# Graph and int8 layers on one core: another way to the quantising maximum, and the next layer's first half among the int8 products

## The chip, the core and the metric

One core of a Trainium2 chip runs the whole program. The number that counts is the device time of one execution in microseconds; three runs of a kernel are timed and their median is given. The profile is of one further execution, taken by the hardware profiler.

## What is computed

The model has four residual steps over 625 rows of 1024 numbers, with 20625 graph edges:

```
x = x + gnn0(layernorm(x))      # relational graph layer, 8 relations, tanh gate
x = x + ffn0(layernorm(x))      # int8 layer, below
x = x + gnn1(layernorm(x))      # h = x @ W.T + b, then a normalised sum over neighbours
x = x + ffn1(layernorm(x))      # top-2 mixture of 8 experts and a shared one
```

The change touches the second step and the start of the third. The second is

```
x_scale = max(abs(x2).max() / 127.0, EPS)            # one maximum over all 625 x 1024
x_int8  = clip(round(x2 / x_scale), -128, 127)
out     = (x_int8 @ weight_int8.T) * x_scale * weight_scale.T + bias
```

so no product of this step can begin before the maximum over all rows of the normalised input is known.

## The kernel before

The 625 rows lie in five chunks (c = 0 to 4) of P = 125 partitions. Each engine has its own program, and `on.wait_ge(*at(event))` waits for a named event of another. An engine works strictly in the order of its program.

**Weights.** Weight tiles (128x512) come in groups of four through two staging buffers (`load`, on SP). ScalarE writes the high part of each tile into a ring of RT = 10 places (`highs(to)`, line 339), and VectorE or, for the tiles in `pool_lo`, GpSimd writes the low part (`lows(to)`, line 349). A group is loaded when the high and low parts of the group two before it exist. A place of the ring is filled again when the product that used it is done. A product in full precision is three matmuls for each of eight tiles (`three`, line 493): 24 for one chunk and one half of the columns. G0 is the first tile of the third step, S1 = G0 + 16 the first of the shared expert.

**PSUM.** Eight banks are handed out in turn by `Banks.take`: the next one that is not held. The one who takes a bank waits for the event that the last user named when it took it. `by_chunk` takes its five banks at its start.

**Gate and norm.** Half 1 of the gate product runs chunk by chunk on TensorE. VectorE takes out each chunk (line 1353), adds it to X (1356), gathers statistics (1164, 1169), takes the row maximum of the chunk before (`row_max`, 1346), and makes the shift of the norm in five one-column steps (`finish`, 1174 to 1183). ScalarE takes the root (899) and writes the normed chunk into U (905); chunk 4's is written by VectorE (1187). GpSimd adds the layer's bias to X after each norm (1807).

**Maximum.** VectorE reduces the five row maxima to a column (1369), TensorE turns the column to a row (606), VectorE reduces the row (1371), TensorE spreads the result over the partitions (612), VectorE makes scale and inverse (1373, 1375).

**Quantising.** ScalarE casts seven of the eight int8 weight tiles to bf16 (1032), once the gate product is done; GpSimd casts the first (1812). VectorE (chunks 0, 2) and ScalarE (1, 3, 4) multiply by the inverse and add a large number that rounds ("q magic", 1379 and 1036); VectorE subtracts it and limits (1382). TensorE turns the chunk in bf16 (623), VectorE writes it to xqT (1387).

**Int8 products.** TensorE runs the chunks' two halves (640). VectorE scales the result (1399), GpSimd adds it to X (1819; chunk 4 on VectorE, 1405), VectorE makes the statistics and the shift of the next norm ("n3"), ScalarE the norm. From chunk 2 on, TensorE turns the normed chunk c - 2 (483); ScalarE writes the high part of the turned chunk (913) and VectorE the low part (1194).

**Third step.** Half 0 of its product (`gnn`, 0) runs by chunk with the turns of chunks 3 and 4 after chunks 0 and 1; then half 1. VectorE takes out each chunk (`g_out`, 1419 and 1422), with ScalarE between (1051), in order of half and chunk, and begins with it after it has made the low parts up to G0 + 17. Then comes the sum over neighbours (668).

## Time and profile before

| | us |
|---|---|
| median of three runs | 1204.71 |
| lowest, highest | 1201.17, 1207.81 |
| the profiled execution | 1205.84 |
| span of its instructions | 1204.1 |

| engine | busy us | share of the span |
|---|---|---|
| TensorE, matmuls | 1111.2 | 92% |
| VectorE | 704.0 | 58% |
| GpSimd | 450.8 | 37% |
| ScalarE | 378.4 | 31% |

Times are microseconds from the start of the span. In the profile PE is TensorE, PEld its loading of weights, DVE VectorE, ACT ScalarE, POOL GpSimd and SP the engine that issues most of the transfers. L1346 is line 1346 of the kernel. "x3" behind a row is the number of instructions that it merges; the time before it is then from the start of the first to the end of the last. A bracket gives how long the engine stood idle before the row and who released it. The granted clock is a share of TensorE's full speed: 1.00 is 2.4 GHz, 0.50 is 1.2 GHz.

### The profile page before, as it was taken

What the parts mean: (1) busy time and instruction counts of PE and PEld (TensorE: products, weight loads), DVE (VectorE), ACT (ScalarE), POOL (GpSimd) and SP (SyncE); (2) the same over time, 40 slices, a digit from 0 to 9 for tenths busy, and PEclk for the clock granted to TensorE, in tenths of its full rate; (3) what the DMA queues carried; (4) which work ended last, traced back from release to release, by engine and by line L of the source; (5) the groups of instructions that cost most, each with busy time, mean ns of one, the idle gap of its engine ahead of it and who ended that gap; (6) DMA issues with size and microseconds to landing.
All of it is one profiled execution on the core that took longest, in us unless ns stands there. A gap on an engine that the chain in (4) does not pass through costs nothing.

```text
span 1204.1 us, 14335 instructions
## 1 busy us (share of the span) xinstructions
PE 1111.2 (92%) x5483; PEld 919.2 (76%) x5483; DVE 704.0 (58%) x1350; ACT 378.4 (31%) x591; POOL 450.8 (37%) x306
## 2 busy tenths in 40 slices
PE   4579999999999999999999999989968997989895
PEld 3467777777777777777799999977746775777773
DVE  6257666665566662121167767666967467656547
ACT  3022222222322222222133233243253324037552
POOL 6006564665556457740033212206544002410006
PEclk9889999999999999999999999989879999978997
DMA  9945577786766556575455663738411102566857
GB/s 351 408 142 142 143 163 195 194 206 190 181 165 148 128 118 146 114 139 190 155 185 170 200 178 105 245 125 210 140 35 53 70 2 72 203 219 232 261 167 244
DMA packets 88179, 202.78 MB, mean 168 GB/s; under 512 B 29383, under 2 KB 45354, under 8 KB 79528
## 3 DMA queue, kind: packets, MB, share of 16 engines
q1 hardware_dynamic: 37962, 129.17, 33.7%
q0 software_dynamic: 32016, 35.50, 13.7%
q10 hardware_dynamic: 18126, 37.13, 10.2%
q8 instruction: 46, 0.75, 0.3%
q14 instruction: 29, 0.24, 0.1%
HBM read 142.37 MB, written 59.39 MB: 168 GB/s over the span
## 4 chain that ended last, share of the span: by engine, by line
PE 80%; DVE 7%; DMA 4%; ACT 2%; issue 1%; POOL 0%; POOLq 0%; DVEq 0%; SPq 0%
PE ps L493 70%; DMA stage<-in_w_e 4%; PE ps L739 3%; PE ps L702 2%; DVE rl L349 1%; PE ps L668 1%; PE ps L750 1%; ACT rh L339 1%; PE ps L685 1%; DVE st L1164 1%; DVE xTl L1194 1%; PE ps L717 1%; ACT EOs L1119 1%; PE ps L483 0%; DVE X L1607 0%
## 5 line engine op out<-in xcount | busy, mean ns | idle before, releaser
L349 DVE TENSOR_TENSOR rl<-stage,rh 128x512 fp32r<-128x512 f32 (+1 forms) x274 | 227.0, 860 | 324.9 <-ACT rh L339 321.2
L493 PE MATMUL ps<-rh,xTh 128*125 128x512 f32 x880 | 351.1, 399 | 24.0 <-DVE xTl L1194 20.0
L339 ACT CAST rh<-stage 128x512 fp32r<-128x512 f32 (+1 forms) x288 | 194.3, 707 | 533.7 <-PE ps L493 310.9
L493 PE MATMUL ps<-rl,xTh 128*125 128x512 f32 x880 | 349.6, 397 | 0.0
L1755 POOL DMA_INDIRECT adj_scratch<-cnt,idx x162 | 266.8, 1647 | 219.0 <-DMA adj_scratch<-cnt,idx 61.2
L493 PE MATMUL ps<-rh,xTl 128*125 128x512 f32 x880 | 347.8, 395 | 0.0
L493 PEld LDWEIGHTS ps<-rh,xTh 128*125 128x125 f32 x880 | 164.4, 187 | 67.7 <-DVE xTl L1194 20.9
L493 PEld LDWEIGHTS ps<-rh,xTl 128*125 128x125 f32 x880 | 164.5, 187 | 42.5
L493 PE MATMUL ps<-rh,Ar 125*125 125x342 f32 x600 | 190.3, 322 | 6.0 <-issue 6.0
L493 PEld LDWEIGHTS ps<-rl,xTh 128*125 128x125 f32 x880 | 164.2, 187 | 40.2
L493 PE MATMUL ps<-rl,Ar 125*125 125x342 f32 x600 | 189.9, 322 | 0.0
L1213 DVE SCALAR_TENSOR_TENSOR EQ<-KR,kc,later 128x768 bf16<-128x768 f32 x162 | 154.3, 1017 | 0.0
L493 PEld LDWEIGHTS ps<-rh,Ar 125*125 125x125 f32 x600 | 113.0, 188 | 6.2 <-issue 6.1
L493 PEld LDWEIGHTS ps<-rl,Ar 125*125 125x125 f32 x600 | 113.0, 188 | 0.0
L1770 POOL TENSOR_TENSOR Atot<-Atot,Ar 128x3125 f32<-128x3125 f32 x7 | 45.4, 6483 | 100.2 <-ACT Ar L935 100.1
L1287 DVE SCALAR_TENSOR_TENSOR U<-ps,rc,U 125x342 f32<-125x342 f32 (+1 forms) x120 | 66.2, 570 | 27.1 <-PE ps L493 24.8
L982 ACT COPY He<-ps 125x512 f32<-125x512 f32 x80 | 46.9, 586 | 30.1 <-PE ps L493 16.5
L349 POOL TENSOR_TENSOR rl<-stage,rh 128x512 fp32r<-128x512 f32 x14 | 17.5, 1273 | 83.8 <-ACT rh L339 83.8
L1194 DVE TENSOR_TENSOR xTl<-ps,xTh 128x500 fp32r<-128x500 f32 x30 | 18.9, 672 | 33.5 <-ACT xTh L913 33.5
L483 PE MATMUL ps<-ident,U 125*128 125x125 f32 x160 | 21.6, 280 | 16.0 <-POOL dms L1736 10.9
L493 PE MATMUL ps<-rh,uTh 128*125 128x512 f32 x80 | 33.5, 419 | 3.0 <-DVE rl L349 2.9
L702 PE MATMUL ps<-xeh,rh 128*128 128x196 f32 x128 | 35.5, 277 | 0.6 <-DVE xel L1588 0.6
(263 smaller groups left out, 1217.4 us busy)
## 6 DMA issues: line engine op xcount, KB each, us to landing
stage<-in_w_rel SPq DMA_DIRECT2D x32, 1024.0 KB, 6.6
stage<-h_scratch SPq DMA_DIRECT2D x24, 855.0 KB, 6.3
stage<-in_w_e SPq DMA_DIRECT2D x16, 1024.0 KB, 6.8
adj_scratch<-Z POOLq DMA_DIRECT2D x16, 767.0 KB, 24.1
KR<-key_scratch ACTq DMA_DIRECT2D x27, 384.0 KB, 3.6
h_scratch<-He ACTq DMA_DIRECT2D x40, 257.0 KB, 9.7
h_scratch<-He ACTq DMA_DIRECT2D x40, 256.0 KB, 8.9
stage<-in_w_gate SPq DMA_DIRECT2D x8, 1024.0 KB, 6.5
```

What stands on the lines that cost most here:

```text
L339: e.copy(h, s).then_inc(*a_hi.up(*[("hi", t) for t in step(i)]))
L349: e.tensor_tensor(l, s, h.bitcast(F32), ALU.subtract).then_inc(*own.up(*[("lo", t) for t in step(i)]))
L483: ins = e.transpose(ps[:, b, j * P:(j + 1) * P], source[:, c, k * 128:(k + 1) * 128], ident[0:P, 0:P])
L493: ins = e.matmul(ps[0:P, b, 0:width], a, m, start=first and n == 0, stop=last and n == len(parts) - 1)
L702: ins = e.matmul(ps[:, b, 0:vn], a[:, ws], m[:, k, v0:v0 + vn], start=k == 0 and j == 0, stop=k == 7 and j == 2)
L739: ins = e.matmul(ps[0:HC, b, :], a, m, start=k == 0 and q == 0, stop=k == 1 and q == 2)
L982: e.copy(He[0:P, s % NHE, 2:514], ps[0:P, banks.of["unit", unit, hf, c], :]).then_inc(*a_out.up(("he", unit, c, hf)))
L1194: e.tensor_tensor(l, ps[:, b, 0:4 * P].rearrange("p (k n) -> p k n", k=4), h.bitcast(F32), ALU.subtract).then_inc(*v_out.up((name, "lo", c ...
L1213: e.scalar_tensor_tensor(out=EQ[:, j, :], in0=KR[:, g % 4, :], scalar=kc[:, t:t + 1], in1=later[:, j0:j0 + TG * 128], op0=ALU.is_equal, op ...
L1287: e.scalar_tensor_tensor(out=U[:, c, to], in0=ps[0:P, b, cols], scalar=rc[:, r, c:c + 1], in1=U[:, c, to], op0=ALU.mult, op1=ALU.add).then ...
L1755: e.indirect_dma_start(accd, bass.IndirectOffsetOnAxis(ap=idx[:, n:n + 1], axis=0), cnt[:, n:n + 1], None, compute_op=ALU.add).then_inc(*d ...
L1770: e.tensor_tensor(flat, flat, arf, ALU.add).then_inc(*p_row.up(("total", r)))
```

## The change

Four things change.

- *The maximum.* The column of row maxima is broadcast to 128 columns and turned once, so that every partition receives the whole row; VectorE reduces it on every partition (to `qs[:, 1:2]`) and makes the scale. The row maximum of chunk 4 is not taken from the normed chunk: `extremes` takes the largest and the smallest of each half of X's chunk 4 before the norm, the four numbers are then multiplied and shifted as the norm would, and the largest magnitude of them is the row maximum. The row maxima of the others stand one iteration earlier, before `finish`.
- *The norm of chunk 4* is written by ScalarE, like the others, ahead of its weight casts.
- *GpSimd* casts the first int8 weight tile first, and then adds the bias to the five chunks, waiting for `extremes` of half 1.
- *The next layer.* `gnn_first(c)` makes chunk c of half 0 and takes its bank when it starts. TensorE's order is now: q 0, q 1, ffn 0, q 2, ffn 1, q 3, ffn 2, turn 0, q 4, ffn 3, gnn 0, turn 1, ffn 4, gnn 1, turn 2, gnn 2, turn 3, gnn 3, turn 4, gnn 4. ScalarE makes the high parts of tiles up to G0 + 7 in one go after "q magic", and those of G0 + 8 and G0 + 9 after turn 4; the low parts of these two go from GpSimd to VectorE.

```diff
--- before.py
+++ after.py
@@ -158,6 +158,7 @@
         deg = sb("deg", [P, 4, C], F32)
         many = sb("many", [1, 1], I32)
         qs = sb("qs", [P, 8], F32)
+        ex = sb("ex", [P, 4], F32)
         triu = sb("triu", [128, 128], F32)
         wt8 = sb("wt8", [P, 8], F32)
         dms = sb("dms", [128, 2 * C], F32)
@@ -316,7 +317,7 @@
         G0, S1, H0 = tile["gnn", 0, 0], tile["s1", 0], tile["h", 0, 0, 0]
         in_h = range(H0, H0 + 3 * C * R)
 
-        pool_lo = [*range(G0 + 2, G0 + 10), *range(S1 + 2, S1 + 8)]
+        pool_lo = [*range(G0 + 2, G0 + 8), *range(S1 + 2, S1 + 8)]
 
         def places(i):
             g, t, rows, width = tiles[i]
@@ -599,18 +600,12 @@
             end_chunks(("gate", 1))
 
 
-            b, freed = banks.take(("q max",), ("q max row",))
+            b, freed = banks.take(("q max",), ("q max all",))
             on.wait_ge(*at("q max column"))
             for ev in freed:
                 on.wait_ge(*at(*ev))
-            e.transpose(ps[0:1, b, 0:P], qs[:, 0:1], ident[0:P, 0:P]).then_inc(*product.up(("q max turned",)))
+            e.transpose(ps[:, b, 0:P], qs[:, 0:1].broadcast_to([P, 128]), ident[0:P, 0:P]).then_inc(*product.up(("q max everywhere",)))
             banks.drop(("q max",))
-            b, freed = banks.take(("q all",), ("q scale",))
-            on.wait_ge(*at("q max row"))
-            for ev in freed:
-                on.wait_ge(*at(*ev))
-            e.matmul(ps[0:P, b, 0:1], onesf[0:1, 0:P], qs[0:1, 1:2], start=True, stop=True).then_inc(*product.up(("q max everywhere",)))
-            banks.drop(("q all",))
 
             def quantised(c):
                 b, freed = banks.take(("q", c), ("q turned", c))
@@ -624,11 +619,7 @@
                 ins.then_inc(*product.up(("q turn", c)))
                 banks.drop(("q", c))
 
-            quantised(0)
-            quantised(1)
-            for c in range(C):
-                if c + 2 < C:
-                    quantised(c + 2)
+            def ffn(c):
                 for hf in range(2):
                     b, freed = banks.take(("ffn", c, hf), ("ffn scaled", c, hf))
                     on.wait_ge(*at("q turned", c))
@@ -640,13 +631,39 @@
                         ins = e.matmul(ps[0:P, b, :], xqT[:, k, c * P:(c + 1) * P], Wb[:, k, HALF[hf]], start=k == 0, stop=k == 7)
                     ins.then_inc(*product.up(("ffn", c, hf)))
                     banks.drop(("ffn", c, hf))
-                if c > 1:
-                    turn("n3", c - 2, U, ("n3", "norm", c - 2))
-
-
-            by_chunk(("gnn", 0), G0, 8, x_stat, lambda c: ("g", c, 0), lambda c: (("n3", "lo", c, 1),),
-                     lambda c: turn("n3", C - 2 + c, U, ("n3", "norm", C - 2 + c)) if c < 2 else None, nothing)
+
+            def gnn_first(c):
+                b, old = banks.take(("gnn", 0, c), ("g", c, 0))
+                for k in range(8):
+                    on.wait_ge(*at("lo", G0 + k))
+                    on.wait_ge(*at("n3", "lo", c, 1))
+                    for ev in old if k == 0 else ():
+                        on.wait_ge(*at(*ev))
+                    ins = three(b, G0 + k, x_stat(k, c), k == 0, k == 7)
+                    done = ([("gnn", 0, c)] if k == 7 else []) + ([("used", G0 + k)] if c == C - 1 else [])
+                    if done:
+                        ins.then_inc(*product.up(*done))
+
+            quantised(0)
+            quantised(1)
+            ffn(0)
+            quantised(2)
+            ffn(1)
+            quantised(3)
+            ffn(2)
+            turn("n3", 0, U, ("n3", "norm", 0))
+            quantised(4)
+            ffn(3)
+            gnn_first(0)
+            turn("n3", 1, U, ("n3", "norm", 1))
+            ffn(4)
+            for c in range(1, C):
+                gnn_first(c)
+                if c + 1 < C:
+                    turn("n3", c + 1, U, ("n3", "norm", c + 1))
             end_chunks(("gnn", 0))
+
+
             by_chunk(("gnn", 1), tile["gnn", 1, 0], 8, x_stat, lambda c: ("g", c, 1), lambda c: (), nothing, nothing)
             end_chunks(("gnn", 1))
             took = [banks.take(("rest", c)) for c in range(C)]
@@ -1021,8 +1038,7 @@
             highs(tile["gate", 1, 0] + RT)
             for c in range(C):
                 root("n2", c)
-                if c < C - 1:
-                    norm("n2", c)
+                norm("n2", c)
 
 
             w8 = lambda k: (W8a if k < 4 else W8b)[:, k % 4, :].bitcast(I8)
@@ -1032,11 +1048,11 @@
                 e.copy(Wb[:, k, :], w8(k)).then_inc(*a_row.up(("wb", k)))
             for c in (1, 3, 4):
                 on.wait_ge(*at("q inverse"))
-                on.wait_ge(*at("row max", c))
+                on.wait_ge(*at("n2", "norm", c))
                 e.activation(U[:, c, :], U[:, c, :], ACT.Identity, bias=magt[:, 0:1], scale=qs[:, 3:4]).then_inc(*a_row.up(("q magic", c)))
             pads("pad again", ("x1", C - 1, 0), ("x1", C - 1, 1))
-            for c in range(C):
-                highs(G0 + 2 + 2 * min(c + 1, 4))
+            highs(G0 + 8)
+            for c in range(C):
                 if c > 1:
                     turned("n3", c - 2, xTh)
                 root("n3", c)
@@ -1345,6 +1361,11 @@
                 on.wait_ge(*at("n2", "norm", c))
                 e.tensor_reduce(sm[:, 4, c:c + 1], U[:, c, :], AX, ALU.max, apply_absolute_value=True).then_inc(*v_row.up(("row max", c)))
 
+            def extremes(hf):
+                on.wait_ge(*at("x1", C - 1, hf))
+                e.tensor_reduce(ex[:, hf:hf + 1], X[:, C - 1, HALF[hf]], AX, ALU.max).then_inc(*v_row.up(("extremes", hf)))
+                e.tensor_reduce(ex[:, 2 + hf:3 + hf], X[:, C - 1, HALF[hf]], AX, ALU.min).then_inc(*v_row.up(("extremes", hf)))
+
             stats("n2", 0, 0, X, ("x1", 0, 0))
             stats("n2", 1, 0, X, ("x1", 1, 0))
             for c in range(C):
@@ -1358,24 +1379,33 @@
                 if c + 2 < C:
                     stats("n2", c + 2, 0, X, ("x1", c + 2, 0))
                 begin("n2", c)
-                if c and c < C - 1:
+                if c:
                     row_max(c - 1)
-                finish("n2", c, X, c < C - 1)
-            row_max(C - 2)
-            row_max(C - 1)
-
-
+                if c == C - 2:
+                    extremes(0)
+                elif c == C - 1:
+                    extremes(1)
+                finish("n2", c, X, True)
+
+
+            on.wait_ge(*at("n2", "shift", C - 1))
+            on.wait_ge(*at("extremes", 1))
+            e.tensor_scalar(ex[:], ex[:], sm[:, 3, C - 1:C], sm[:, 2, C - 1:C], ALU.mult, ALU.add).then_inc(*v_row.up(("extremes normed",)))
+            on.wait_ge(*at("extremes normed"))
+            e.tensor_reduce(sm[:, 4, C - 1:C], ex[:], AX, ALU.max, apply_absolute_value=True).then_inc(*v_row.up(("row max", C - 1)))
             on.wait_ge(*at("row max", C - 1))
+            on.wait_ge(*at("row max", C - 2))
             e.tensor_reduce(qs[:, 0:1], sm[:, 4, :], AX, ALU.max).then_inc(*v_row.up(("q max column",)))
-            on.wait_ge(*at("q max turned"))
-            e.tensor_reduce(qs[0:1, 1:2], ps[0:1, banks.of["q max",], 0:P], AX, ALU.max).then_inc(*v_out.up(("q max row",)))
             on.wait_ge(*at("q max everywhere"))
-            e.tensor_scalar(qs[:, 2:3], ps[0:P, banks.of["q all",], 0:1], 1.0 / 127.0, EPS, ALU.mult, ALU.max).then_inc(*v_out.up(("q scale",)))
+            e.tensor_reduce(qs[:, 1:2], ps[0:P, banks.of["q max",], 0:P], AX, ALU.max).then_inc(*v_out.up(("q max all",)))
+            on.wait_ge(*at("q max all"))
+            e.tensor_scalar(qs[:, 2:3], qs[:, 1:2], 1.0 / 127.0, EPS, ALU.mult, ALU.max).then_inc(*v_row.up(("q scale",)))
             on.wait_ge(*at("q scale"))
             e.reciprocal(qs[:, 3:4], qs[:, 2:3]).then_inc(*v_row.up(("q inverse",)))
             for c in range(C):
                 if c in (0, 2):
                     on.wait_ge(*at("q inverse"))
+                    on.wait_ge(*at("n2", "norm", c))
                     e.tensor_scalar(U[:, c, :], U[:, c, :], qs[:, 3:4], MAGIC, ALU.mult, ALU.add).then_inc(*v_row.up(("q magic", c)))
                 on.wait_ge(*at("q magic", c))
                 on.wait_ge(*at("gate", 1, C - 1))
@@ -1403,13 +1433,14 @@
                         on.wait_ge(*at("ffn scaled", c, hf))
                         on.wait_ge(*at("x plus fbias", c))
                         e.tensor_tensor(X[:, c, HALF[hf]], X[:, c, HALF[hf]], U[:, c, HALF[hf]], ALU.add).then_inc(*v_row.up(("x2", c, hf)))
+                if c == 0:
+                    lows(G0 + 8)
                 if c > 1:
                     turned("n3", c - 2, xTh, xTl)
                 for hf in range(2):
                     stats("n3", c, hf, X, ("x2", c, hf))
                 begin("n3", c)
                 finish("n3", c, X, c < C - 1)
-            lows(G0 + 10)
 
 
             def g_out(c, hf):
@@ -1801,15 +1832,14 @@
                 on.wait_ge(*at("z gap", c))
                 on.wait_ge(*at("x plus xn", c))
                 e.tensor_tensor(X[:, c, HALF[0]], X[:, c, HALF[0]], U[:, c, HALF[0]], ALU.add).then_inc(*p_row.up(("x1", c, 0)))
-            for c in range(C):
-                on.wait_ge(*at("n2", "norm", c))
-                on.wait_ge(*at("fbias"))
-                e.tensor_tensor(X[:, c, :], X[:, c, :], BB[:], ALU.add).then_inc(*p_row.up(("x plus fbias", c)))
-
-
             on.wait_ge(*at("w8"))
             on.wait_ge(*at("gate", 1, C - 1))
             e.tensor_copy(Wb[:, 0, :], W8a[:, 0, :].bitcast(I8)).then_inc(*p_row.up(("wb", 0)))
+            for c in range(C):
+                on.wait_ge(*at("n2", "norm", c))
+                on.wait_ge(*at("extremes", 1))
+                on.wait_ge(*at("fbias"))
+                e.tensor_tensor(X[:, c, :], X[:, c, :], BB[:], ALU.add).then_inc(*p_row.up(("x plus fbias", c)))
             split[0] = G0 + 2
             for c in range(C):
                 if c < C - 1:
```

## Rows read from the trace of the kernel before

**Rows 1.** Table of stretches; columns: us, busy (instructions) by engine, clock, DMA, GB/s

```profile
800.00:900.00 100.00, 86.35 (x398) 65.72 (x398) 77.75 (x124) 39.18 (x56) 47.15 (x31) 0.88 0.39 114
```

**Rows 2.** Timeline of TensorE, 864 to 925; start us, us, instruction, idle before it

```profile
880.30 0.37 PE L606 MATMUL ps<-ident,qs 125*1 125x125 f32 x1 [7.41 <-DVE qs L1369]
881.03 0.57 PE L612 MATMUL ps<-qs,onesf 1*125 1x1 f32 x2 [0.37 <-DVE qs L1371]
...
887.37 6.56 PE L640 MATMUL ps<-Wb,xqT 128*125 128x512 bf16 x16 [0.77 <-DVE xqT L1387]
```

**Rows 3.** Timeline of VectorE, 864 to 950

```profile
875.11 0.21 DVE L1169 BATCH_NORM_AGGREGATE mv<-st 125x2 f32<-125x12 f32 x1
...
877.71 2.34 DVE L1346 TENSOR_REDUCE sm<-U 125x1 f32<-125x1024 f32 x2
...
881.84 0.16 DVE L1375 RECIPROCAL qs<-qs 125x1 f32<-125x1 f32 x1
...
886.64 1.85 DVE L1387 TENSOR_SCALAR xqT<-ps 128x1000 bf16<-128x1000 bf16 x3
```

**Rows 4.** Timeline of ScalarE, 855 to 950

```profile
872.70 1.24 ACT L905 ACTIVATE U<-X,sm 125x1024 f32<-125x1024 f32 x1 [1.76 <-DVE sm L1183]
...
875.55 2.92 ACT L1032 CAST Wb<-W8a 128x1024 bf16<-128x1024 int8 x3
...
882.16 3.50 ACT L1036 ACTIVATE U<-U,magt,qs 125x1024 f32<-125x1024 f32 x3
...
885.77 1.12 ACT L339 CAST rh<-stage 128x512 fp32r<-128x512 f32 x2
```

**Rows 5.** Timeline of GpSimd, 840 to 960

```profile
869.67 2.40 POOL L1807 TENSOR_TENSOR X<-X,BB 125x1024 f32<-125x1024 f32 x1 [2.29 <-ACT U L905]
...
877.87 2.34 POOL L1807 TENSOR_TENSOR X<-X,BB 125x1024 f32<-125x1024 f32 x1 [1.33 <-DVE U L1187]
```

**Rows 6.** Timeline of all engines, 992 to 995 and 1007 to 1011

```profile
992.44 2.52 POOL L349 TENSOR_TENSOR rl<-stage,rh 128x512 fp32r<-128x512 f32 x2 [73.80 <-ACT rh L339]
...
992.47 1.28 DVE L1180 SCALAR_TENSOR_TENSOR sm<-sm 125x1 f32<-125x1 f32 x1
...
993.78 1.19 DVE L1183 SCALAR_TENSOR_TENSOR sm<-mv,sm 125x1 f32<-125x1 f32 x1
...
1008.74 1.74 DVE L1187 TENSOR_SCALAR U<-X,mv,sm 125x1024 f32<-125x1024 f32 x1
```

**Rows 7.** Timeline of TensorE again, the waits among the int8 products

```profile
907.32 1.08 PE L483 MATMUL ps<-ident,U 125*128 125x125 f32 x8 [1.29 <-ACT U L905]
908.24 3.62 PE L640 MATMUL ps<-Wb,xqT 128*125 128x512 bf16 x16
914.21 1.07 PE L483 MATMUL ps<-ident,U 125*128 125x125 f32 x8 [2.35 <-ACT U L905]
...
921.23 0.62 PE L483 MATMUL ps<-ident,U 125*128 125x125 f32 x4 [0.38 <-DVE U L1399]
922.93 0.65 PE L483 MATMUL ps<-ident,U 125*128 125x125 f32 x4 [1.08 <-DVE xTl L1194]
```

**Rows 8.** Timeline of VectorE again, chunk 2 scaled and low part 0

```profile
906.50 1.40 DVE L1399 SCALAR_TENSOR_TENSOR U<-ps,qs,BA 125x512 f32<-125x512 f32 x2
908.81 1.26 DVE L1194 TENSOR_TENSOR xTl<-ps,xTh 128x500 fp32r<-128x500 f32 x2 [0.90 <-ACT xTh L913]
```

**Rows 9.** Chain that ended last, 925 to 962; start us, us, what

```profile
929.97 32.24 PE ps L493 x139
```

**Rows 10.** Timeline of VectorE, 948 to 960, outputs of the half's first chunks

```profile
950.62 0.68 DVE L1419 TENSOR_TENSOR U<-ps,BA 125x512 f32<-125x512 f32 x1
...
957.05 0.68 DVE L1419 TENSOR_TENSOR U<-ps,BA 125x512 f32<-125x512 f32 x1
```

**Rows 11.** Table of stretches of one microsecond; columns as in rows 1

```profile
876.00:877.00 1.00, 0.00 (x0) 0.00 (x0) 0.89 (x4) 1.00 (x2) 0.54 (x1) 0.60 0.03 8
893.00:894.00 1.00, 1.00 (x9) 0.67 (x8) 0.04 (x1) 0.00 (x0) 0.17 (x1) 0.87 0.00 0
```

## The prediction

> **What bounds the kernel now.** Read the table of stretches first. TensorE is nearly always busy, but in the hundred microseconds that hold the end of the gate product, the int8 layer and the start of the next layer it is idle for 13.65 us and its mean granted clock is 0.88 [rows 1]. So the change touches one of the few places with idle TensorE time to win. Then TensorE's timeline there: the gate product ends at 872.9 us; it waits 7.41 us for the column of row maxima, turns and broadcasts the maximum, and starts the int8 products at 887.37 [rows 2]. The others' timelines say why. VectorE takes 2.34 us for the last two row maxima from 877.71 and has the inverse scale at 882.0 [rows 3]. ScalarE, released from the last root at 875.6, casts seven int8 weight tiles until 882.16 (6.61 us), then makes three of the five "q magic" passes in 3.50, the last ending at 885.66 [rows 4]. The last quantising and the first transposed chunk follow, and TensorE starts 1.71 us after the last pass. Two chains therefore run side by side up to 887.4: the maximum (VectorE) and casts plus passes (ScalarE), and the second is only just covered by the first. A change that shortens the first wins nothing if it lengthens the second.
>
> After that TensorE stands still four times among the int8 products and the turns of the next layer's input: 1.29, 2.35, 0.38 and 1.08 us, in all 5.10 [rows 7]; from 929.97 on it runs without a gap [rows 9].
>
> **Part 1: the maximum.** Removed: a row maximum of 1024 elements (half of 2.34 us, pitch about 1.09) behind the last norm, the last norm on VectorE, and the second small product (0.67 us of waiting on VectorE) [rows 2, 3]. Added: four reductions of 512 elements; the trace has none, the nearest row is the 1024 one, so between half (0.55) and all (1.1) of it, and I take 0.57, since the time follows the elements. A short multiply-add on four numbers and a reduction on four (0.16 to 0.20 each, like the reciprocal at 881.84). Iteration 3 of VectorE's loop is lengthened by 1.15 but no longer meets GpSimd's bias additions, so VectorE reaches the last gate chunk within 0.1 us of before; its aggregate, at 875.11 before, comes at about 875.2, or 875.5 if the GpSimd cast that now starts at 872.95 delays one addition. Then row maximum 3 (1.09), both extremes (1.15): done at 877.6 to 877.9. With five short steps of 0.2 the shift would be ready at 878.9 and the inverse scale at 880.7, 1.3 us earlier than before. That is the gain meant.
>
> **Part 2: what is queued on ScalarE.** The last norm moves from VectorE to ScalarE, and in ScalarE's order it stands before the seven casts. It waits for the shift of chunk 4. Before, the casts began at 875.55, after the last root; now they wait for shift plus norm (1.24, of which the next overlaps 0.1) [rows 4]. So: casts begin 1.18 after the shift, +6.61 for the casts, +3.50 for three passes, +1.38 for the last quantising (0.61), its transposed chunk until TensorE starts (886.64 to 887.37) and a hand-over [rows 2, 3]. TensorE's int8 start = shift + 12.7. With the shift at 878.9 this is 891.6, 4.2 us later than 887.37. The gain of part 1 is not on the chain that ends last.
>
> **Part 3: GpSimd's additions.** Before, the five additions of the bias (2.4 us each) came one after each norm (the third and the fifth of them stand in [rows 5]). Now GpSimd casts a weight first, and the additions wait for the extremes of chunk 4: four of them are ready at once and run back to back from 877.7, just when VectorE makes the shift of chunk 4. What such an overlap does is in the trace [rows 6]: GpSimd runs two tensor_tensor of 1.26 us back to back from 992.44; a one-column scalar_tensor_tensor of VectorE with two inputs in SBUF, normally 0.16, starts at 992.47 and takes 1.28; the next takes 1.19. Each ends as one GpSimd instruction ends: the two alternate, one VectorE instruction for each GpSimd one. A tensor_scalar of 0.81 takes 1.74 in the same way; reductions beside GpSimd do not stretch (2.34 for two at 877.71 beside the addition at 877.87) [rows 3, 5]. The finish of chunk 4 has four such steps with two SBUF inputs, and GpSimd has four additions of 2.40 to put against them. Shift: 877.9 + 4 x 2.40 = 887.5. If the first of the four just gets in ahead, three waits remain, 885.1; GpSimd's record would begin some 0.02 us ahead, and in rows 6 a lead of 0.03 was enough, so I take four. TensorE's int8 start is then 887.5 + 12.7 = 900.2, **12.8 us** later than before (bounds: +4.2 with no such waits, +10.4 with three; if a sixth instruction got in the way, +15.2).
>
> The Trainium skill ("SBUF — State Buffer", Who interferes with whom) says that a tensor_scalar that runs in a 2-port mode also contends, and that the one that issues first keeps the pair for the whole instruction. The trace shows it only for a 1024-wide tensor_scalar [rows 6]; for the four-wide one of the extremes no run here shows it. By that rule it would wait for one more addition where three waits came before; the shift, which ScalarE's chain hangs on, would not move, nor would the sum.
>
> **Part 4: the woven order.** The first half of the next layer for chunk 0 goes between ffn 3 and ffn 4. VectorE's order is the old one, so it still takes transposed chunk 4, then scales chunk 2 (at 906.50 before), then forms low part 0 (ending at 910.07, some 0.9 earlier once the casts in front of it on ScalarE are gone) [rows 8]. TensorE is done with ffn 3 at about 906.3 on this scale and waits 2.9 us for that low part. From chunk 2 on each product stands directly behind its own turn: the low part is ready 1.88 us after the time at which TensorE could go on (turn from 907.32, next product 908.24 before, low part 910.07) [rows 7, 8]. Three times gives 5.6. New idle: 8.5 us, against 5.6 for the old gaps counted the same way (5.10 plus the overlap of about 0.15 at each gap). **+2.9 us**; between 0 (high and low parts hidden for half of them) and +5. The low parts of tiles G0+8 and G0+9 move from GpSimd to VectorE, done after turn 4 beside the last product of the half (5.55 us): nothing. ScalarE's six early casts (1.12 for two) [rows 4] lie beside ffn 0: nothing; each would show in full only if ffn 0 hid them no longer. The loads on SP follow the low parts as before.
>
> **Part 5: the PSUM banks.** The banks are handed out in turn. Written out for the new order, gnn half 0 holds banks 5, 2, 6, 1, 7 (chunks 0 to 4, the first gate chunk in bank 0), and half 1 takes banks 0 to 4. Chunk 1 of half 1 gets bank 1, which frees only when VectorE has taken out chunk 3 of half 0. In the old order chunks 0 and 1 of half 1 had banks that turns had left, and chunk 2 waited only for chunk 0. VectorE starts those outputs late, after the low parts of the ring at 950.62, and needs 2.15 us for each; chunk 3 is out at 957.73 [rows 10]. TensorE, with 0.2315 us a product and 24 in a chunk (5.55), counted from 929.97, reaches chunk 1 of half 1 at 952.2 [rows 9]. Nothing in the order that gates VectorE's start (the ring's tiles, used by chunk 4 of half 0, and the load behind them) comes nearer. **+5.6 us** of idle TensorE; between 0, if the outputs begin earlier than I count, and 6.5. Such a gap costs clock too. After the stop at 872.9 the granted clock fell to its 1.2 GHz level within the microsecond from 876 (mean 0.60), some 3.3 us after the stop, and was back at 2.4 GHz soon after 893 (0.87), 5.9 us after the products began at 887.37 [rows 2, 11]. Sixteen products take 6.56 at the low level and 3.62 at the high one [rows 2, 7], so 45% of the time at the low level is lost: 5.9 us cost 2.65. I take **+2.2**, nearer that row; the lower end is 0.
>
> **Sum.** 12.8 + 2.9 + 5.6 + 2.2 = 23.5 us. The profiled execution had 1205.84 (span 1204.1); it would be 1229.3. The median of the runs was 1204.71, 1.1 less: forecast 1228 us, with its own range 1221 to 1235. Nothing later takes it back: from 975 on every stage waits for TensorE's products.
>
> **Rivals.** (a) *Only the queue costs, the port does not.* If GpSimd's additions start later, or VectorE gets in between them, the term falls to 4.2: 1220. For it: never were four additions in a row against four dependent small steps in this trace; against it: rows 6 show two in a row strictly alternating. Chance 0.12. (b) *The bank wait does not show* (VectorE's outputs start early enough): 1228 - 7.8 = 1220. Chance 0.10. (c) *The change does what it says:* the maximum is 1.3 us earlier, ScalarE's casts do not wait (or are overtaken by slack that I miscounted) and the weave covers the four gaps: -1.3 - 5.1, about 1198. It decides if the casts start before 877. Chance 0.05. (d) *About even:* ScalarE's 4.2 is paid, the weave gives back as much, no port or bank wait: 1205. Chance 0.07. (e) *Worse than counted:* the first wait on the port holds and the clock stays low through the half after the bank wait, or a later bank is late too: +8, 1236. Chance 0.06. The forecast keeps 0.60.
>
> **How the numbers follow.** Range: forecast, (a) and (b) hold 0.82; widened at the top for the clock, 1213 to 1236. Here 0.5% is 6 us, about what a measurement can tell from no change. Faster by more than that: (c), 0.05. Within: (d), 0.07. Slower: the rest, 0.88.
>
> **What would show it.** In the changed profile: ScalarE's seven casts start at 888 to 889 and not at 875.6; four scalar_tensor_tensor of one column on VectorE near 878 to 887 take about 2.4 us each, each ending with an addition on GpSimd; TensorE's int8 products begin near 900; a gap of about 3 us before the woven chunk 0 and three of 1.9 ahead of chunks 2, 3 and 4; a gap of 5 to 6 us between chunks 0 and 1 of half 1, released by VectorE's output, with low clock behind it. The prediction is wrong if the casts start before 880, if the small steps stay at 0.16 us, or if half 1 runs without a gap.

## The result, and the profile after

The changed kernel takes 1227.6 us (median of four runs, 1226.4 to 1230.3) against 1204.2 before: ratio 1.0196, 95% interval 1.0163 to 1.023. Its profiled execution took 1230.3, with a span of 1228.5.

Page of the changed kernel, busy time by engine, and its table of stretches:

```profile
PE 1118.8 (91%) x5481; PEld 924.8 (75%) x5481; DVE 714.4 (58%) x1357; ACT 380.0 (31%) x592; POOL 450.0 (37%) x304
...
800.00:900.00 100.00, 74.19 (x337) 58.04 (x337) 81.04 (x116) 40.73 (x59) 41.67 (x27) 0.84 0.38 115
900.00:1000.00 100.00, 84.98 (x375) 63.62 (x374) 49.22 (x93) 24.62 (x40) 17.41 (x14) 0.91 0.14 48
```

TensorE's idle time in the first stretch has grown from 13.65 to 25.8 us [rows 1]; in the second it is 15.0. The last three numbers of a row of this table are TensorE's granted clock, the share of the DMA engines and GB/s.

Timeline of TensorE, changed kernel (start us, us, instruction, idle before it and releaser); it answers to [rows 2] and [rows 7]:

```profile
888.76 0.47 PE L607 MATMUL ps<-ident,qs 125*128 125x125 f32 x1 [14.81 <-DVE qs L1398]
...
899.00 6.21 PE L631 MATMUL ps<-Wb,xqT 128*125 128x512 bf16 x16 [2.16 <-DVE xqT L1417]
...
913.99 1.07 PE L484 MATMUL ps<-ident,U 125*128 125x125 f32 x8 [0.98 <-ACT U L922]
...
922.77 0.76 PE L494 MATMUL ps<-rh,xTh 128*125 128x512 f32 x1 [3.81 <-DVE xTl L1210]
...
943.28 0.49 PE L494 MATMUL ps<-rh,xTh 128*125 128x512 f32 x1 [1.54 <-DVE xTl L1210]
```

The gate product ends at 873.95. The column of maxima comes 14.81 us later (7.41 before), and the int8 products start 25.05 us after the end of the gate product (14.48 before). Then follow gaps of 0.98 and 3.81 us, and three of 1.54 (the other two at 951.54 and 959.75).

Timeline of VectorE, changed kernel, against [rows 3]:

```profile
878.25 0.67 DVE L1367 TENSOR_REDUCE ex<-X 125x1 f32<-125x512 f32 x1
878.85 0.15 DVE L1190 RECIPROCAL sm<-sm 125x1 f32<-125x1 f32 x1
879.03 0.16 DVE L1192 SCALAR_TENSOR_TENSOR sm<-mv,sm 125x1 f32<-125x1 f32 x1
879.22 2.19 DVE L1194 SCALAR_TENSOR_TENSOR sm<-sm 125x1 f32<-125x1 f32 x1
881.45 2.26 DVE L1196 SCALAR_TENSOR_TENSOR sm<-sm 125x1 f32<-125x1 f32 x1
883.75 2.26 DVE L1199 SCALAR_TENSOR_TENSOR sm<-mv,sm 125x1 f32<-125x1 f32 x1
886.04 2.28 DVE L1393 TENSOR_SCALAR ex<-ex,sm 125x4 f32<-125x4 f32 x1
888.36 0.16 DVE L1395 TENSOR_REDUCE sm<-ex 125x1 f32<-125x4 f32 x1
...
889.59 0.15 DVE L1402 TENSOR_SCALAR qs<-qs 125x1 f32<-125x1 f32 x1
...
905.70 0.68 DVE L1417 TENSOR_SCALAR xqT<-ps 128x1000 bf16<-128x1000 bf16 x1 [6.15 <-PE ps L618]
```

Timelines of GpSimd and ScalarE, changed kernel, against [rows 4, 5]:

```profile
874.11 1.04 POOL L1837 CAST Wb<-W8a 128x1024 bf16<-128x1024 int8 x1 [20.56 <-PE ps L494]
879.06 11.54 POOL L1842 TENSOR_TENSOR X<-X,BB 125x1024 f32<-125x1024 f32 x5 [3.92 <-DVE sm L1190]
...
886.04 1.24 ACT L922 ACTIVATE U<-X,sm 125x1024 f32<-125x1024 f32 x1 [9.05 <-DVE sm L1199]
887.19 2.92 ACT L1048 CAST Wb<-W8a 128x1024 bf16<-128x1024 int8 x3
890.02 3.88 ACT L1048 CAST Wb<-W8b 128x1024 bf16<-128x1024 int8 x4
893.80 3.50 ACT L1052 ACTIVATE U<-U,magt,qs 125x1024 f32<-125x1024 f32 x3
```

GpSimd's additions run back to back from 879.06, 2.30 us apart. VectorE's instructions at 879.22, 881.45, 883.75 and 886.04 end 2.35, 4.65, 6.95 and 9.26 us after that, each with one addition; in a1 below, without the additions, they take 0.16 to 0.29. The reduction at 888.36 and the one-column tensor_scalar at 889.59 lie beside the fifth addition and are not stretched. ScalarE stands 9.05 us for the shift, then makes norm, seven casts and three passes.

Chain that ended last and timeline of VectorE, changed kernel, half 1 (against [rows 9, 10]):

```profile
976.77 25.25 PE ps L494 x96
1002.03 8.17 PE ps L685 x35
...
969.61 0.68 DVE L1450 TENSOR_TENSOR U<-ps,BA 125x512 f32<-125x512 f32 x1
...
976.04 0.68 DVE L1450 TENSOR_TENSOR U<-ps,BA 125x512 f32<-125x512 f32 x1
```

The output at 976.04 is that of chunk 3 of half 0. Chunk 1 of half 1 starts when it ends, after 5.61 us of idle TensorE. The 96 products behind the gap take 25.25 us instead of 22.2 (96 x 0.2315).

Granted clock (last but two) in single microseconds of the changed kernel, around both gaps:

```profile
921.00:922.00 1.00, 0.00 (x0) 0.00 (x0) 1.00 (x3) 0.76 (x2) 1.00 (x1) 0.63 0.00 0
...
928.00:929.00 1.00, 1.00 (x6) 0.79 (x5) 0.00 (x0) 0.00 (x0) 1.00 (x2) 0.96 0.99 410
...
975.00:976.00 1.00, 0.00 (x0) 0.00 (x0) 0.63 (x1) 0.34 (x1) 0.00 (x0) 0.93 0.00 0
976.00:977.00 1.00, 0.23 (x1) 0.23 (x2) 0.72 (x2) 0.24 (x1) 0.00 (x0) 0.50 0.00 0
```

The clock fell to 1.2 GHz in both gaps: in the first (TensorE idle from 918.96) at about 921.3, in the second (idle from 971.16) at about 975.9. It was back at 2.4 GHz at about 928.0, so behind the first gap the 24 products of chunk 0 take 8.26 us instead of 5.55.

To compare kernels whose early parts shift by a microsecond or two, I take three moments of each profiled execution: end of the gate product, start of the int8 products (A is the time between them), start of the sum over neighbours as the chain that ended last has it (B is the time from the int8 start to it).

| kernel | A | B | A + B | ratio to before, interval |
|---|---|---|---|---|
| before | 14.48 | 87.18 | 101.7 | |
| the same, profiled again | 14.48 | 86.81 | 101.3 | |
| changed | 25.05 | 103.03 | 128.1 | 1.0196 (1.0163 to 1.023) |
| the same, profiled again | 25.05 | 102.84 | 127.9 | |
| a1 additions back | 19.46 | 100.33 | 119.8 | 1.0152 (1.0131 to 1.0173) |
| a2 casts first | 21.77 | 103.13 | 124.9 | 1.0186 (1.0169 to 1.0203) |
| a3 both | 17.94 | 102.71 | 120.7 | 1.0151 (1.0127 to 1.0174) |
| a4 other bank | 25.05 | 94.86 | 119.9 | 1.0134 (1.0116 to 1.0153) |
| a5 turns early | 25.05 | 99.86 | 124.9 | 1.0198 (1.0169 to 1.0227) |
| a6 maximum alone | 25.04 | 85.84 | 110.9 | 1.008 (1.0054 to 1.0107) |
| a7 woven order alone | 14.48 | 102.91 | 117.4 | 1.0152 (1.0122 to 1.0182) |
| b1 | 14.48 | 86.86 | 101.3 | 0.9995 (0.9976 to 1.0013) |
| b3 | 14.48 | 81.38 | 95.9 | 0.9964 (0.9948 to 0.9979) |
| b2 | 12.11 | 80.97 | 93.1 | 0.9912 (0.989 to 0.9935) |

From the start of the sum over neighbours to the end the same instructions run, and the profiled executions take 223 to 230 us for them: 229.5 and 226.1 for the kernel before, 226.5 and 225.5 for the changed one. That scatter is why A + B, and not the span, is used below.

B has a scatter of its own, from the moment at which the clock comes back behind the int8 start. That is 5.9 us after the start in the kernel before (893.3), 5.2 in the changed kernel, and 3.2 to 3.3 in a6 and b3, where the order of work in that stretch is that of before. The low level costs half of the time at it, so that B of the kernel before is 1.3 us longer than that of a6 or b3 by this alone (an estimate from these clocks; the first turn of the next layer's input starts 19.95 us after the int8 start in the kernel before, 18.65 in a6 and 18.62 in b3).

### The profile page after: what moved, and what is told of

Its sections match the earlier page's. It is cut to its first block, busy times and chain, and to the rows that moved or that the text cites. A ratio compares the mean times of both kernels' runs of the same rounds, so it can differ in the third digit from the quotient of the medians.

```text
span 1228.5 us, 14333 instructions
## 1 busy us (share of the span) xinstructions
PE 1118.8 (91%) x5481; PEld 924.8 (75%) x5481; DVE 714.4 (58%) x1357; ACT 380.0 (31%) x592; POOL 450.0 (37%) x304
## 4 chain that ended last, share of the span: by engine, by line
PE 77%; DVE 9%; DMA 4%; ACT 3%; issue 1%; POOL 0%; POOLq 0%; DVEq 0%; SPq 0%; ACTq 0%
PE ps L494 67%; DMA stage<-in_w_e 3%; PE ps L756 2%; PE ps L719 2%; DVE rl L350 2%; PE ps L685 1%; DVE st L1180 1%; PE ps L767 1%; PE ps L631 1%; DVE xTl L1210 1%; ACT rh L340 1%; PE ps L702 1%; PE ps L734 1%; ACT Wb L1048 1%; PE ps L484 1%
## 5 line engine op out<-in xcount | busy, mean ns | idle before, releaser
L494 PE MATMUL ps<-rh,xTh 128*125 128x512 f32 x880 | 354.7, 403 | 36.4 <-DVE xTl L1210 27.1
L1786 POOL DMA_INDIRECT adj_scratch<-cnt,idx x162 | 269.9, 1666 | 221.8 <-DMA adj_scratch<-cnt,idx 80.4
L719 PE MATMUL ps<-xel,rh 128*128 128x196 f32 x128 | 35.4, 277 | 0.0
```

Source lines behind the costliest of these rows:

```text
L494: ins = e.matmul(ps[0:P, b, 0:width], a, m, start=first and n == 0, stop=last and n == len(parts) - 1)
L719: ins = e.matmul(ps[:, b, 0:vn], a[:, ws], m[:, k, v0:v0 + vn], start=k == 0 and j == 0, stop=k == 7 and j == 2)
L1786: e.indirect_dma_start(accd, bass.IndirectOffsetOnAxis(ap=idx[:, n:n + 1], axis=0), cnt[:, n:n + 1], None, compute_op=ALU.add).then_inc(*d ...
```

## Experiments

**Undo one cause of A at a time.** The woven order stays in a1 to a3. In a1 GpSimd's additions for chunks 0 to 3 stand behind their norms again, and only the last waits for the extremes:

```diff
-            on.wait_ge(*at("w8"))
-            on.wait_ge(*at("gate", 1, C - 1))
-            e.tensor_copy(Wb[:, 0, :], W8a[:, 0, :].bitcast(I8)).then_inc(*p_row.up(("wb", 0)))
             for c in range(C):
+                if c == C - 1:
+                    on.wait_ge(*at("w8"))
+                    on.wait_ge(*at("gate", 1, C - 1))
+                    e.tensor_copy(Wb[:, 0, :], W8a[:, 0, :].bitcast(I8)).then_inc(*p_row.up(("wb", 0)))
+                    on.wait_ge(*at("extremes", 1))
                 on.wait_ge(*at("n2", "norm", c))
-                on.wait_ge(*at("extremes", 1))
```

> The changed kernel with GpSimd's bias additions of chunks 0 to 3 back behind their own norms, as in the kernel before; then the weight cast; only chunk 4's addition waits for the extremes. All else is as changed. Theory (the port): the three one-column steps of chunk 4's shift that took 2.2 us each shrink to about 0.16, the shift is ready near 879.7 instead of 886.0, ScalarE's casts start near 881 and TensorE's int8 products near 892.4 instead of 899.0: 6.6 us less than the changed kernel, about 1221. Rival (only the queue on ScalarE costs, the stretched steps are merely waiting for something else): the start stays within 1 us of 899.0 and the time near 1227.6.

Timeline of VectorE, a1:

```profile
878.71 0.16 DVE L1196 SCALAR_TENSOR_TENSOR sm<-sm 125x1 f32<-125x1 f32 x1
878.91 0.16 DVE L1199 SCALAR_TENSOR_TENSOR sm<-mv,sm 125x1 f32<-125x1 f32 x1
879.11 0.29 DVE L1393 TENSOR_SCALAR ex<-ex,sm 125x4 f32<-125x4 f32 x1
...
881.05 2.34 DVE L1409 TENSOR_SCALAR U<-U,qs 125x1024 f32<-125x1024 f32 x1
```

The same instructions on the same data are back to 0.16 and 0.29 us, and A falls by 5.6. What stretches them is the additions beside them. The last addition (880.49, 2.35 us) now meets a 1024-wide multiply, which takes 2.34 for 0.75. The last three steps of the shift take 0.55 us instead of 6.79, 6.24 less; VectorE reaches the aggregate of chunk 4 0.63 later after the end of the gate product (3.13 against 2.50), again with additions beside its loop. That makes the 5.6. The casts begin 7.64 us after the end of the gate product against 13.24.

B is 2.7 shorter as well, though the edit changes nothing there. The clock accounts for it: 0.4 behind the int8 start, 0.9 behind the gap of 3.79 (24 products in 7.36 us instead of 8.26), 1.3 behind the bank wait (96 in 23.92 instead of 25.25).

In a2 the additions stay as changed, and ScalarE writes the norm of chunk 4 behind its casts:

```diff
             for c in range(C):
                 root("n2", c)
-                norm("n2", c)
+                if c < C - 1:
+                    norm("n2", c)
...
                 e.copy(Wb[:, k, :], w8(k)).then_inc(*a_row.up(("wb", k)))
+            norm("n2", C - 1)
```

> The changed kernel with ScalarE's seven weight casts ahead of the norm of chunk 4; GpSimd's additions stay where the change put them. Theory: the casts run from about 877 to 883.6 beside the stretched steps, the norm follows the shift at 886, the inverse scale comes at 890 as before, the three passes run from 890 to 893.5 and TensorE's int8 products start near 895: 4 us less than the changed kernel, about 1223.5. Rival (the port alone carries the loss and the queue costs nothing): start stays near 899, 1227.6.

Timeline of ScalarE, a2:

```profile
874.40 2.92 ACT L1049 CAST Wb<-W8a 128x1024 bf16<-128x1024 int8 x3
877.23 3.88 ACT L1049 CAST Wb<-W8b 128x1024 bf16<-128x1024 int8 x4
883.56 1.24 ACT L922 ACTIVATE U<-X,sm 125x1024 f32<-125x1024 f32 x1 [2.45 <-DVE sm L1201]
887.49 3.51 ACT L1054 ACTIVATE U<-U,magt,qs 125x1024 f32<-125x1024 f32 x3 [2.69 <-DVE qs L1406]
```

The casts now run beside the stretched steps (still 2.19 to 2.27 us each), but the passes wait for the inverse, which these steps delay. A falls by only 3.3. The chain of the maximum has become the later one. With both undone (a3):

> Both together: additions behind their norms and casts ahead of the norm of chunk 4. Theory: casts 877 to 883.6, norm of chunk 4 at once behind them, three passes from 884.8 to 888.2, int8 products from about 889.6: 9.4 us less than the changed kernel, about 1218, and still some 1 us later than in the kernel before, since the norm that VectorE made before now stands on ScalarE, the longer chain. Rival (the new maximum shows its full 1.3 us once both are undone): start near 886.5, about 1215.

A falls by 7.1, less than the 8.9 of a1 and a2 together, and 3.5 remain. They are in the rows: the casts begin 3.80 us after the end of the gate product against 2.66 before (1.1), the norm on ScalarE stands ahead of the passes (1.1), and one quantising step meets the last addition (timeline of VectorE, a3):

```profile
885.52 1.88 DVE L1414 TENSOR_SCALAR xq<-U 125x1024 bf16<-125x1024 f32 x1 [2.67 <-ACT U L1054]
```

It takes 1.88 for 0.69 (1.2), beside GpSimd's addition at 884.50. I had expected none of the 1.2.

**Undo one cause of B.** a4 differs from the changed kernel in one line: half 1 of the third step begins with the bank of the last turn.

```diff
             end_chunks(("gnn", 0))
+            banks.turn = banks.of["n3", "turn", C - 1, 0]
```

> The changed kernel; only the bank with which half 1 of the next layer's product begins is set by hand, to the one that the turn of chunk 4 left, so that its five chunks get banks whose last users are low parts 4, 4 and the outputs of chunks 0, 2, 4 of half 0. No wait is removed, no other bank moves. Theory (the bank): the gap of 5.61 us ahead of chunk 1 of half 1 goes, and with it the low clock behind it (96 matmuls in 25.25 us instead of 22.2): 8.6 us less, about 1219. Rival (VectorE's late outputs hold up half 1 whatever the bank): the gap stays at a later chunk, within 2 us of 1227.6.

Chain that ended last, a4:

```profile
958.54 33.67 PE ps L494 x144
992.21 7.84 PE ps L686 x34
```

The last chunk of half 0 and all of half 1 run without a gap and at the full clock (144 x 0.234). A + B falls by 8.2, which is 5.6 of wait and 2.6 of clock. VectorE's outputs come no earlier in a4: the first is at 968.25 against 969.61, and a4's gate product ends 1.65 earlier. Only whose bank is waited for has changed.

In a5 the three bf16 turns of chunks 2 to 4 stand one product earlier, as in the order before:

```diff
             quantised(1)
+            quantised(2)
             ffn(0)
-            quantised(2)
+            quantised(3)
             ffn(1)
-            quantised(3)
+            quantised(4)
             ffn(2)
             turn("n3", 0, U, ("n3", "norm", 0))
-            quantised(4)
             ffn(3)
```

> The changed kernel with TensorE's bf16 turns of chunks 2, 3 and 4 each one int8 product earlier, as in the kernel before (q 2 before ffn 0, q 3 before ffn 1, q 4 before ffn 2); the woven chunk 0 and all the rest as changed. In the changed kernel VectorE takes transposed chunk 2 before it scales chunk 0, and that turn now comes only after ffn 0, so its work on chunk 0 ends 13.7 us after ffn 0's start instead of 11.7. Theory (this is the part of the weave's loss that my sum missed): the gap of 3.81 us ahead of the woven chunk 0 shrinks to about 2, the granted clock stays high there (24 matmuls in 5.6 us instead of 8.3), and the time falls by 4 to 5 us, to about 1223. Rival (the gap is set by GpSimd's or ScalarE's work on the ring's tiles): gap and time unchanged.

Timeline of TensorE, a5:

```profile
919.57 0.47 PE L494 MATMUL ps<-rh,xTh 128*125 128x512 f32 x1 [3.17 <-DVE xTl L1210]
...
920.33 0.51 PE L494 MATMUL ps<-rh,xTh 128*125 128x512 f32 x1
920.64 0.63 PE L494 MATMUL ps<-rl,xTh 128*125 128x512 f32 x1
```

The woven chunk starts 21.60 us after the int8 start instead of 23.77, and B falls by 3.2. The gap of 0.98 ahead of the first turn has gone. The gap ahead of the woven chunk shrinks only from 3.81 to 3.17, where about 2 was expected, as TensorE comes to it earlier too, and the clock still falls: the 24 products take 7.38 us. The 0.9 between that and 8.26 is part of the 3.2, but a1 has the same 0.9 without this edit, so that only some 2.3 are the edit's. The ratio does not show the 3 us (1.0198 against 1.0196, intervals of 3 to 4 us to either side); the trace does.

**Each half of the change alone.** a6 has the new maximum, the norm of chunk 4 on ScalarE and GpSimd's new order, but TensorE's order and the making of the weights' high and low parts are those of before:

```diff
+            for c in range(C):
+                if c + 2 < C:
+                    quantised(c + 2)
...
-            ffn(2)
-            turn("n3", 0, U, ("n3", "norm", 0))
-            quantised(4)
-            ffn(3)
-            gnn_first(0)
...
+                if c > 1:
+                    turn("n3", c - 2, U, ("n3", "norm", c - 2))
```

a7 is the kernel before with the same lines edited the other way round: the old maximum and the woven order.

> The changed maximum, the norm of chunk 4 on ScalarE and GpSimd's new order, with TensorE's order, the high parts and the low parts of the kernel before. Theory: from the end of the gate product to the first int8 product 25.1 us as in the changed kernel (14.5 before), then the old course with its four short gaps and no gap in half 1: about 10.6 us over the kernel before, ratio 1.009. Rival (the two parts of the change feed each other, so that the maximum alone costs less than 8 or more than 13).

> The kernel before with the woven order alone (TensorE's order, high and low parts as changed); the old maximum. Written out, its half 1 gets the same wait: chunk 1's bank is that of chunk 3 of half 0. Theory: first int8 product 14.5 us after the gate product as before; gaps of 1, 3.8 and three times 1.5 us and low clock behind the second, 7 us; the bank's gap of 5.6 and 3 us of low clock: 16 us over the kernel before, ratio 1.013. Rival (the weave only loses because the int8 products start late): ratio within 1.005.

a6 gives A + B = +9.2, all of it in A (B is 1.3 shorter); a7 gives +15.7, all in B, with A at 14.48 to the hundredth. Timeline of TensorE, a7:

```profile
888.56 6.17 PE L636 MATMUL ps<-Wb,xqT 128*125 128x512 bf16 x16 [1.93 <-DVE xqT L1409]
...
912.26 0.76 PE L493 MATMUL ps<-rh,xTh 128*125 128x512 f32 x1 [3.80 <-DVE xTl L1216]
...
966.18 0.79 PE L493 MATMUL ps<-rh,xTh 128*125 128x512 f32 x1 [5.52 <-DVE U L1442]
```

The two gaps of the changed kernel (3.81 and 5.61) stand in it, as do the three of 1.54. So the woven order causes them whatever the maximum does. 9.2 and 15.7 make 24.9 of 26.4. Of the 1.5 left over, 1.3 is the clock behind the int8 start, which came back sooner in a6 than in the kernel before; without it the two halves make 26.2.

**Can the four gaps of before be closed?** b1 keeps the kernel before and moves the turns of chunks 2 to 4 of the next layer's input one chunk back:

```diff
-                if c > 1:
+                if c in (2, 3):
                     turn("n3", c - 2, U, ("n3", "norm", c - 2))
...
-                     lambda c: turn("n3", C - 2 + c, U, ("n3", "norm", C - 2 + c)) if c < 2 else None, nothing)
+                     lambda c: turn("n3", 2 + c, U, ("n3", "norm", 2 + c)) if c < 3 else None, nothing)
             end_chunks(("gnn", 0))
+            banks.turn = banks.of["gnn", 0, C - 1] + 1
```

> A version meant to gain: the kernel before, in which only the turns of chunks 2, 3 and 4 for the next layer stand one chunk later (behind chunks 0, 1 and 2 of half 0), so that each has a product of 5.5 us between itself and the chunk that needs it and another ahead of it; the first bank of half 1 is set to the one behind half 0's last, so that chunks 0 to 2 of half 1 get the turns' banks. No product is moved between int8 products. Theory: of the gaps 1.29, 2.35, 0.38, 1.08 only the first stays; about 4 us less than before, 1198 to 1200 against a kernel before of 1202 to 1204 (ratio 0.9965). Rival (the norms on VectorE and ScalarE are what is late, and the gap moves behind): ratio 1.000.

No difference, where 4 us were expected. Three of the four gaps have gone (the first, 1.28, is left) and one of another kind has come, timeline of TensorE, b1:

```profile
919.79 1.10 PE L483 MATMUL ps<-ident,U 125*128 125x125 f32 x4 [2.63 <-DVE U L1400]
```

The turn of chunk 2 has got the bank of the last int8 product, and waits 2.63 us until VectorE has scaled it; 24 products behind it take 6.63 us instead of 5.55, at the low clock. b3 gives the banks of that product to chunks 3 and 4 of half 0, which come later:

```diff
+                    if name == ("gnn", 0) and c in (0, 3):
+                        banks.turn = banks.of["ffn", C - 1, 0] + (0 if c else 2)
+                    took.append(banks.take((*name, c), freed(c)))
...
+            banks.turn = banks.of["ffn", C - 1, 0] + 5
```

> The kernel before with the turns of chunks 2, 3 and 4 one chunk later, as in b1, and other banks for half 0: chunks 3 and 4 take the two banks that ffn 4 used (emptied late), chunks 0 to 2 and the turns take banks emptied earlier; half 1 begins with the turns' banks. In b1 the turn of chunk 2 stood 2.63 us, released by VectorE's scaling of chunk 4, whose bank it had been handed, and the clock went low behind it. Theory (again a bank, not late work): that gap and the low clock go, only the 1.3 us ahead of turn 1 stays, about 4 us less than before, ratio 0.9965. Rival (the norm of chunk 2 is what is late): the gap stays near 2 us and the ratio near 1.000.

B is 5.8 shorter than before, and of the gaps only the first (1.31) is left. 1.3 of the 5.8 is the clock behind the int8 start, which the edit does not touch; what is left, 4.5, agrees with the ratio (0.9964, some 4.3 us) and with the 4 expected. b2 adds three things to b3: the maximum by the one turn of the repeated column, but over five row maxima as before; chunk 0 limited (line 1382 before) and taken to xqT before chunks 2 to 4 are limited; bf16 turns 2 to 4 behind products 0 to 2, taken by VectorE behind the scalings.

```diff
-            e.transpose(ps[0:1, b, 0:P], qs[:, 0:1], ident[0:P, 0:P]).then_inc(*product.up(("q max turned",)))
+            e.transpose(ps[:, b, 0:P], qs[:, 0:1].broadcast_to([P, 128]), ident[0:P, 0:P]).then_inc(*product.up(("q max everywhere",)))
...
-            e.matmul(ps[0:P, b, 0:1], onesf[0:1, 0:P], qs[0:1, 1:2], start=True, stop=True).then_inc(*product.up(("q max everywhere",)))
...
-                if c + 2 < C:
-                    quantised(c + 2)
                 for hf in range(2):
...
+                if c + 2 < C:
+                    quantised(c + 2)
...
+            limited(0)
+            limited(1)
             quantised(0)
+            limited(2)
...
```

> b3 and two more steps. The single turn of a repeated column for the maximum (the change's first step, alone; the row maxima, the norm of chunk 4, ScalarE's and GpSimd's order as before). And VectorE quantises chunk 0 and takes its transposed form before it goes on to chunks 2 to 4, with TensorE's bf16 turns of chunks 2, 3, 4 behind ffn 0, 1, 2 and VectorE taking them behind the scalings, so that ffn 0 waits for chunk 0 and the weights alone. Theory: inverse scale 0.65 us earlier, first int8 product about 12 us after the gate product instead of 14.5, in all 6 to 7 us less than before, ratio 0.9945. Rival (ScalarE's casts, done 9.4 us after the gate product, and its passes still set the start): start within 0.5 us of 14.5, ratio 0.9965.

0.9912 (0.989 to 0.9935), faster than either kernel and by more than the 6 to 7 us expected. A + B is 8.6 shorter than before; 1.1 of that is again the clock behind the int8 start (back 3.7 us after it). Chain that ended last, b2:

```profile
874.92 6.71 ACT Wb L1031 x7
881.63 1.15 ACT U L1035
...
883.55 1.02 PE ps L621 x8
...
926.37 38.98 PE ps L493 x168
```

A is 12.11, and it now ends with ScalarE's casts and its first pass, no longer with the maximum; the gap ahead of the first turn has shrunk to 0.26. The inverse starts 8.43 us after the end of the gate product (880.69), against 8.95 before. How the 2.4 us that A gains divide between the single turn and the order of the chunks, no run separates.

The last two kernels are before and changed once more, for the scatter of a profiled execution:

> The kernel before once more, for a second profile. From the end of the gate product to the first product of the neighbour sum 101.66 us in the first profile, from there to the end 229.55; the changed kernel 128.08 and 226.5, and the experiments 223.3 to 229.0 for the latter. Theory (the tail scatters between executions and has nothing to do with the change): 101.7 within 0.5 again, tail anywhere from 223 to 230. Rival (the change gives 3 us back later): tail again near 229.5.

> The changed kernel once more. Theory: 128.1 us within 1 from the gate product's end to the neighbour sum, with the same gaps; tail from 223 to 230. Rival: tail again near 226.5 whatever the kernel before shows.

Their rows repeat the first ones: A at 14.48 and 25.05, the gaps 3.80 and 5.64.

## Why the prediction was right, and where its sizes were off

**Part 1, the gain meant.** Forecast 1.3 us, and the rows bear that out, but no run shows it whole. In the changed kernel the extremes end 4.97 us after the gate product (878.92 less 873.95), within the 4.7 to 5.0 counted. In a1, where nothing blocks what follows them, the inverse starts 2.6 us after their end (878.23 to 880.85). The two make 7.6 against 8.95 before, a gain of 1.3 to 1.4 (an estimate from these rows). a1 itself gets 0.7 (8.24, 880.85 less 872.61), since with the additions behind their norms VectorE's loop is 0.63 longer. So in these runs the additions cost either the loop or the shift. b2 gets 0.5 from the single turn alone.

**Part 2, the queue on ScalarE.** Right: int8 start = end of shift (886.01) + 12.99, forecast 12.7; the 0.3 is from the last pass to TensorE, 1.70 as before, which the sum had at 1.38. a2 shows that undoing the queue alone brings 3.3.

**Part 3, the additions.** Right in kind, in place and in the step of one instruction for one addition; off by one wait. The sum took four waits and the lower bound three, +10.4; measured +10.6 with three. The fourth stretched instruction was the tensor_scalar of the extremes and not a step of the shift. The step at 879.03 got in 0.03 us ahead of the first addition at 879.06. In a6 and in the changed kernel profiled again the same step is the one that gets in. That was a choice between two bounds on a lead of 0.02, and the rows gave too little ground for it: in rows 6 it was GpSimd that led by 0.03, here VectorE did.

The sentence on the Trainium skill ("SBUF — State Buffer", Who interferes with whom) agrees with the trace in what it says of the wait: the four-wide tensor_scalar of the extremes took 2.28 us beside an addition (886.04) and 0.29 without (a1). That it ran in such a mode, no row shows. It was off the chain of ScalarE, as said; in a2, where the chain of the maximum is the last one, it counts.

**Part 4, the woven order.** Right that the weave costs more idle time than it saves. The term is mis-sized: +2.9 forecast, some +7 measured, where its bounds were 0 and +5. From the table: B grew by 15.85, of which 5.61 and 3.0 are the bank wait and its clock, which leaves 7.2. The gaps sum to 0.98 + 3.81 + 3 x 1.54 = 9.41 against 5.10 [rows 7], +4.3 where 2.9 was forecast; the forecast had none, 2.9, and three of 1.88. The other 2.7 is the low clock behind the gap of 3.81, for which the sum had nothing. So the idle time alone is within the bounds, and the clock takes the term out of them. Two causes. First, "VectorE's order is the old one" was true, but not TensorE's: the bf16 turn of chunk 2 now stands behind product 0. VectorE, which takes that turn ahead of scaling chunk 0, stood 6.15 us until 905.70, and everything behind it came later. Low part 0 was ready 23.6 us after the int8 start, where 22.7 - 0.9 was counted. a5 undoes this, and the woven chunk starts 2.2 us sooner. Second, the clock loss had been priced behind one gap and not behind the other.

**Part 5, the bank.** Right: 5.61 against 5.6, and clock 3.0 against 2.2. The row of before, 2.65, was nearer; and as the last of its sixteen products already ran at the high level (granted clock 0.87 in the microsecond from 893 [rows 11]), its 45% is too small: half of 5.9 us is 2.9. a4 removes both with one line.

**Sum.** 10.6 + 4.3 + 2.7 + 5.6 + 3.0 = 26.2 of the 26.4 us that A + B grew; forecast 23.5. The errors are -2.2 in part 3, +4.1 in part 4 and +0.8 in part 5, of both signs. The median grew by 23.4, and the interval of the ratio allows 19.6 to 27.7, so that the forecast of 1228 met 1227.6 to within 0.4 us owes something to luck. As to the rivals, (a) asked for small steps at 0.16 us, and they take 2.2; (b) asked for no gap in half 1, and it is 5.6; (c) and (d) asked for casts before 877 or a weave that gives back, and the casts begin at 887.19; (e) adds 8 us to the sum, and A + B shows 2.9 of it.

**What stays open.** Behind gaps of the same length the loss of clock differs: 24 products behind the gap ahead of the woven chunk took 7.36 us in a1 and 8.16 to 8.42 in the changed kernel, a2, a3, a4 and a7. The 96 behind the bank wait took 23.92 in a1 and 25.2 to 25.3 in the others. The table of stretches shows what the loss consists of, granted clock (last but two) in single microseconds of a1:

```profile
916.00:917.00 1.00, 1.00 (x6) 0.81 (x5) 0.85 (x2) 0.00 (x0) 1.00 (x2) 0.96 0.00 0
...
920.00:921.00 1.00, 1.00 (x6) 0.77 (x5) 0.41 (x1) 0.36 (x1) 1.00 (x1) 0.84 0.68 246
```

In a1 the clock fell only at 916.9, when the products that began at 915.41 had been running for 1.5 us, and was back at 920.3. In the changed kernel it fell at 921.3, inside the gap, and was back at 928.0, 5.3 us after the products began at 922.77. So products ran at the low level for 3.4 and 5.3 us, and half of that, 1.7 and 2.6, is about what they lost (1.8 and 2.7). What decides when the clock falls and when it comes back, no run here was made to tell.

## What to carry to other kernels

Before an operation is moved to another moment, look for what the other engine does in that moment: a queue of 2.3 us additions on GpSimd cost a chain of VectorE steps of 0.16 us one addition for each step. That held for one-column scalar_tensor_tensor with both inputs in SBUF and for the four-wide tensor_scalar, not for reductions. Where banks are handed out in turn, write out who had each bank last and when he lets it go; one line that sets the turn was worth 8 us here, and one more choice of banks made the difference between b1, which gained nothing, and b3. When a chain is to be shortened, find the one that ends just before it: it is the ceiling of the gain, and lengthening it costs in full.

## What the runs showed of the hardware that was not expected

- The order in which the two engines met was the same each time: in the changed kernel, profiled twice, and in a6 the same one-column step slips in 0.03 us ahead of the additions, and A is 25.04 to 25.05 each time, also in a4 and a5.
- TensorE's clock fell in a gap as short as 2.63 us (b1, 0.82 in the microsecond from 919, 0.50 in the next) and not in one of 2.35 [rows 7], behind which the products ran at their full pace. A gap of 3.8 us cost another 1.8 to 2.9 us in clock, that of 5.6 cost 1.7 to 3.0: nearly as much, so a gap's price isn't proportional to its length. In the changed kernel the clock fell 2.3 us into the gap of 3.81 and 4.7 us into that of 5.61, in a1 only 1.5 us after the gap.
- Among VectorE's small instructions beside an addition, the four-wide tensor_scalar took 2.28 us (886.04), while the one-column one at 889.59 took 0.15 and the reductions their usual 0.16. The first has both its factors in SBUF columns, the second takes constants; no run tells whether width or operands make the difference.
